# Fused dilated attention and mixture of experts on one core: ScalarE takes one of four masked key blocks, value products run in pairs of segments, one-hot rows come by a GpSimd transfer

## The chip, the core and the metric

The kernel runs on one core of a Trainium2 chip. The metric is the time of one execution on the device in microseconds. The core has five engines that matter here: TensorE (PE) multiplies, VectorE (DVE), ScalarE (ACT) and GpSimd (POOL) do element-wise work, and SyncE (SP) mostly issues transfers. Every engine runs its own instruction list strictly in order; semaphores tie the lists together.

## The reference, cut to what matters

The input is x, 4 batches of 512 tokens of width 128, in float32. Attention has 16 heads of width 8; tokens are put in a snake order, cut into 4 segments of 128, and each query sees every second key of its own segment, so 64 keys.

```python
x = x + layernorm(attn(layernorm(x), w_qkv, w_out))
x = x + layernorm(ffn(layernorm(x), ...))

# attn, per batch, head and segment
scores = einsum('bhsqd,bhskd->bhsqk', qh * scale, kd)   # 128 queries, 64 keys
o = einsum('bhsqk,bhskd->bhsqd', softmax(scores), vd)
return o_in_order @ w_out.T

# ffn: 8 experts, each token uses the best two, plus a shared gated path
combine = zeros.at[rows, topi].add(topw)
h = silu(einsum('nd,edf->nef', xf, w1)); ye = einsum('nef,efd->ned', h, w2)
return einsum('ne,ned->nd', combine, ye) + sigmoid(xf @ gate_w) * shared
```

All eight experts are computed for all tokens and weighted by `combine`.

## The kernel before, in words

The program is written as five instruction lists, one for each engine. Small functions emit one step for one batch `b` (and, in attention, for one segment `s` or one half of the heads); at the end of each engine's part a long hand-set sequence of calls fixes the order. Nothing is scheduled at run time: what stands first in an engine's list runs first, and a wait blocks all behind it.

Stages of one batch in attention:

- `x_T`, `k_project`, `q_project`, `values` (PE) project the normalised input. `k_high`/`q_high` (ACT) and `k_low`/`q_low` (DVE) split each projection in a high and a low part. For batches 1 to 3 SP places the parts on partitions 0 to 95 of `Ks` and `Qs` (`k_place`, `q_place`, L257 to L268).
- `k_blocks` (DVE, L1478 to L1486) multiplies `Ks` by a column of `cst` that is one for the rows of one head of a group and zero elsewhere; it does so four times a batch (`HG` is 4) and writes the masked key blocks `Kb`. Batch 0 uses `k_blocks_0` on two halves.
- `scores_q` (PE, L532) forms scores with queries on partitions; `maxima` (DVE, L1501) takes the negated row maxima from one PSUM bank of two; `max_split` (L1508, L1510) puts them in `Mq`; `max_T` (PE, L541) transposes them, and `max_rows` (ACT L1020, DVE L1493) writes them in rows 96 to 127 of `Qs`.
- `scores_k` (PE, L555) forms the scores again with keys on partitions. It uses all 128 rows: rows 96 to 127 of `Kb` are one-hot over the heads, so the product already holds score minus maximum. The one-hot rows are made by ACT (`key_ones`, L1094, in `kone`) and copied by SP into both halves of `Kb` (L274).
- `exps` (ACT, L1078) takes the exponential of one half's bank into one of four buffers `Pr`. `attend` (PE, L572) multiplies by the values for one segment: eight products on strips of 32 columns. `attended` (ACT, L1070) copies the 256 columns to `AVs`, `attend_T` (PE, L585) transposes them, and `divide` (DVE, L1517 and L1519) divides two segments at a time.
- `output_T`, `project` (PE), `y_copy` (ACT), statistics (DVE), powers and the residual `TR` (POOL) give the input of the second half.

In the second half PE runs `expert_h` (L443 to L445, three products for each hidden layer) and `expert_o` (L676) for eight experts and the shared path; for the last batch these are `last_h` and `last_o` (L731) on halves of the tokens. ACT applies SiLU and weights experts 1, 3, 5 and the shared path (`weight`); DVE adds the other experts (`accumulate`, L1619; `last_sum`, L1650); POOL adds ACT's parts (L377, L385) and computes exponentials of the router for batches 2 and 3 (`router_exp`, L332). Batches overlap: PE works on `scores_k` of one batch, `scores_q` of the next, and from batch 2 on the experts of batch 0.

The first steps of the program: ACT loads `cst`, makes the two parts of the selection matrix `sel` (L1212, L1213), then `kone` (L1094), and only then copies the first half of the transposed input (`x_copy_0`, L974).

## Time and profile before

| | us |
|---|---|
| median of 3 runs | 146.08 (145.68 to 146.86) |
| the profiled execution, as timed | 146.6 |
| its span, from the first to the last instruction | 144.8 |
| PE busy | 134.2 (93%) |
| DVE busy | 125.8 (87%) |
| ACT busy | 106.2 (73%) |
| POOL busy | 58.0 (40%) |

The profiled execution took 1.8 us more than its span, and 0.5 us more than the median. A PE instruction's shown duration reaches into the next one's, since matmuls are pipelined; the chain of waits, which lays pieces end to end, tells better what a group of matmuls costs. An idle time in brackets is what an engine waited before an instruction, with the one that released it.

### The profile page before, as it was taken

How to read it: one execution, taken by the hardware profiler on the slowest of the kernel's cores; microseconds unless marked ns; L12 is line 12 of the kernel's file. 1: busy time of each engine (PE TensorE's matmuls, PEld its weight loads, DVE VectorE, ACT ScalarE, POOL GpSimd, SP SyncE). 2: the span in 40 equal slices, each digit the busy share in tenths (PEclk: the TensorE clock that was granted, in tenths of full speed). 3: DMA queues.
4: the chain of work that ended last, by engine and by line, in shares of the span. 5: the costliest groups of instructions: out<-in, count | busy, mean ns of one | idle time of the engine just before them, and what ended most of it. 6: DMA issues, size and time to landing. Idle time of an engine off the chain costs nothing.

```text
span 144.8 us, 3566 instructions
## 1 busy us (share of the span) xinstructions
PE 134.2 (93%) x1142; PEld 117.0 (81%) x1142; DVE 125.8 (87%) x478; ACT 106.2 (73%) x264; POOL 58.0 (40%) x57
## 2 busy tenths in 40 slices
PE   6889988999999999999999999999999999999940
PEld 5578775887978688878889799999789899999930
DVE  6969999999899899979789684999999949999892
ACT  4569786876896478658989893675588777977670
POOL 7343023000039533704532009949533498305221
PEclk9999999999999999999999999999999999999996
DMA  4941089999993860000000000000000200020022
GB/s 139 264 108 38 32 172 136 247 181 158 196 302 114 142 77 5 0 0 7 0 2 5 0 0 0 5 2 0 0 2 5 72 2 2 2 71 5 0 72 72
DMA packets 13217, 9.54 MB, mean 66 GB/s; under 512 B 1040, under 2 KB 12048, under 8 KB 13200
## 3 DMA queue, kind: packets, MB, share of 16 engines
q1 hardware_dynamic: 12784, 9.12, 29.9%
q10 hardware_dynamic: 416, 0.21, 0.5%
q8 instruction: 9, 0.15, 0.4%
q14 instruction: 8, 0.07, 0.2%
HBM read 3.69 MB, written 1.05 MB: 33 GB/s over the span
## 4 chain that ended last, share of the span: by engine, by line
PE 76%; DVE 8%; ACT 5%; issue 4%; DMA 3%; POOL 1%; POOLq 1%; ACTq 0%; DVEq 0%
PE bank L676 14%; PE bank L555 10%; PE bank L532 7%; PE bank L443 6%; PE bank L572 6%; PE bank L445 5%; PE bank L444 5%; PE bank L731 4%; DMA cst<-in_consts 3%; PE bank L585 2%; PE bank L605 2%; PE bank L503 2%; PE bank L541 2%; DVE negm L1501 1%; PE bank L617 1%
## 5 line engine op out<-in xcount | busy, mean ns | idle before, releaser
L357 POOL TENSOR_TENSOR RS<-VE,nhalf 128x4 f32<-128x4 f32 x14 | 15.4, 1099 | 50.8 <-DVE VE L1405 50.8
L1501 DVE TENSOR_REDUCE negm<-bank 128x8 f32<-128x512 f32 x32 | 21.1, 686 | 1.8 <-PE bank L532 1.4
L1078 ACT ACTIVATE Pr<-bank 128x512 f32<-128x512 f32 x32 | 18.8, 600 | 4.0 <-PE bank L555 3.8
L1619 DVE SCALAR_TENSOR_TENSOR X<-bank,CW,X 128x128 f32<-128x128 f32 x60 | 16.7, 341 | 4.5 <-PE bank L676 4.5
L555 PE MATMUL bank<-Qs,Kb 128*128 128x128 f32 x128 | 19.3, 278 | 0.4 <-ACT Pr L1078 0.3
L555 PEld LDWEIGHTS bank<-Qs,Kb 128*128 128x128 f32 x128 | 16.7, 190 | 3.0 <-issue 1.6
L676 PEld LDWEIGHTS bank<-w2n,Pr 128*128 128x128 f32 x128 | 15.8, 191 | 0.9 <-issue 0.2
L443 PE MATMUL bank<-XH,w1h 128*128 128x512 f32 (+1 forms) x40 | 16.2, 406 | 0.2 <-ACT Pr L1143 0.2
L676 PE MATMUL bank<-w2n,Pr 128*128 128x128 f32 x128 | 16.4, 276 | 0.0
L332 POOL TENSOR_TENSOR EX<-base,DL 128x36 f32<-128x36 f32 x2 | 12.2, 6124 | 9.3 <-DVE DL L1554 9.3
L1158 ACT ACTIVATE Tm<-bank,CW 128x128 f32<-128x128 f32 x36 | 10.2, 370 | 6.6 <-PE bank L676 4.8
L532 PE MATMUL bank<-Kb,Qs 96*128 96x256 f32 x64 | 14.2, 318 | 0.1
L445 PE MATMUL bank<-XL,w1h 128*128 128x512 f32 (+1 forms) x40 | 14.0, 349 | 0.0
L444 PE MATMUL bank<-XH,w1l 128*128 128x512 f32 (+1 forms) x40 | 13.9, 349 | 0.0
L1143 ACT ACTIVATE Pr<-bank 128x512 f32<-128x512 f32 x19 | 11.2, 604 | 2.2 <-PE bank L445 1.4
L532 PEld LDWEIGHTS bank<-Kb,Qs 96*128 96x128 f32 x64 | 9.4, 189 | 2.1 <-issue 1.5
L572 PE MATMUL bank<-Pr,Vb 128*32 128x128 f32 x256 | 10.3, 279 | 0.1
L1070 ACT ACTIVATE AVs<-bank 128x256 f32<-128x256 f32 x16 | 6.2, 386 | 5.2 <-PE bank L572 5.2
L377 POOL TENSOR_TENSOR Tm<-Tm 128x512 f32<-128x512 f32 x6 | 7.7, 1277 | 4.7 <-ACT Tm L1158 4.6
L731 PE MATMUL bank<-w2n,Pr 128*128 128x128 f32 x64 | 8.8, 275 | 0.0
L443 PEld LDWEIGHTS bank<-XH,w1h 128*128 128x128 f32 x40 | 7.6, 190 | 1.3 <-ACT Pr L1143 0.6
L1484 DVE TENSOR_SCALAR Kb<-Ks,cst 96x1024 fp32r<-96x1024 f32 x12 | 8.3, 745 | 0.1
(155 smaller groups left out, 346.2 us busy)
## 6 DMA issues: line engine op xcount, KB each, us to landing
Qs<-qch SPq DMA_DIRECT2D x6, 256.0 KB, 5.5
Kb<-kone SPq DMA_DIRECT2D x8, 128.0 KB, 4.9
X<-in_L_attn_x SPq DMA_DIRECT2D x4, 256.0 KB, 6.3
XP<-in_x_snake SPq DMA_DIRECT2D x3, 256.0 KB, 4.3
Ks<-kch SPq DMA_DIRECT2D x6, 128.0 KB, 3.1
Qs<-qcl SPq DMA_DIRECT2D x3, 256.0 KB, 7.2
out<-XN SPq DMA_DIRECT2D x3, 256.0 KB, 2.2
w1n<-in_L_ffn_w SPq DMA_DIRECT2D x1, 512.0 KB, 8.7
```

The lines of the kernel that those rows point to most:

```text
L357: nc.gpsimd.tensor_tensor(RS[:, k, b], VE[:, k, b], nhalf[:], ALU.pow).then_inc(pw[k], 1)
L443: mm(out_, wh, vh, start=True, stop=False)
L444: mm(out_, wl, vh, start=False, stop=False)
L445: return mm(out_, wh, vl, start=False, stop=True)
L532: i = mm(S1[n % 2][:, j * 256:(j + 1) * 256], Qs[0:MROW, b % 2, g, s * P:(s + 1) * P], Kb[0:MROW, b % 2, g, s], start=True, stop=True)
L555: i = mm(S2[s2_bank(n)][:, j * P:(j + 1) * P], Kb[:, b % 2, g, s, 2 * pr:2 * pr + 2], Qs[:, b % 2, g, s * P:(s + 1) * P], start=True, stop ...
L572: i = mm(PC[j * VW:(j + 1) * VW, (s % 2) * 2 * P + half * P:(s % 2) * 2 * P + (half + 1) * P], Vb[:, b % 2, s, half * 4 + j], Pr[:, n % 4, ...
L676: i = mm(ps[output_bank(n, s)][:, s * P:(s + 1) * P], lhs[:, s * P:(s + 1) * P], w, start=True, stop=True)
L731: i = mm(ps[(6, 7, 5)[j]][:, s * P:(s + 1) * P], hs[:, j, c + s * P:c + (s + 1) * P], w2n[:, u % E], start=True, stop=True)
L1078: A(Pr[:, n % 4], bank(S2[s2_bank(n)], 4), ACT.Exp).then_inc(S["ex"], 1)
L1501: V.tensor_reduce(negm[:, b % 2, s, 8 * half:8 * half + 8], bank(S1[n % 2], 8, KEYS), AX.X, ALU.max, negate=True).then_inc(S["mx"], 1)
L1619: V.scalar_tensor_tensor(out=acc[:, b, t], in0=ps[output_bank(n)][:, t * P:(t + 1) * P], scalar=CW[:, b, t, k:k + 1], in1=acc[:, b, t], op ...
```

## The change

1. **One-hot rows.** `key_ones` on ACT, the tile `kone` and SP's eight copies are gone. The rows come as a new input `key_rows` in DRAM (32 rows of 16 KB) by two transfers that POOL issues: `key_heads(0)` behind `powers(0, 1)`, `key_heads(1)` behind `powers(0, 3)`, the second waiting for the placed queries of batch 1. `cst` is 16 columns narrower.
2. **Key blocks.** For batches 1 to 3 DVE makes three of the four blocks, and ACT the fourth (`k_block`), from the same `Ks`.
3. **Value products in pairs.** `attend`, `attended` and `attend_T` handle two segments at a time: 16 products in one run on a whole PSUM bank, one copy of 512 columns. `Pr` has six buffers for `exps` instead of four.
4. **Early loads.** On SP `w1n`, `woT` and `X` of batches 0 and 1 come ahead of `k_place(1)`.
5. **New orders** of the calls on all engines. In the start `x_T_0(1)` goes ahead of `qkv_0(0)`, and the second part of `sel` behind the first copy of the transposed input. At the end `finish(1)` (DVE) goes from between the sums of batch 2 to behind `norm_out(2)`, `finish_out(1)` (ACT) to behind `last_silu(10)`, and POOL's `powers(3, 1)` to behind `add_weighted(2)`.

```diff
+            def key_heads(u):
+                if u:
+                    pool.wait_ge(q_in[1], 16 * PARTS)
+                pool.dma_start(Kb[MROW:P, u].rearrange("p g s h k -> p (g s h k)"), key_rows).then_inc(kdma[u], 16)
...
-            key_ones(0)
+            sp.dma_start(w1n[:], w1.rearrange("e d f -> d e f")).then_inc(S["ld_w1"], 16)
+            sp.dma_start(woT[:], w_outT).then_inc(S["ld_wout"], 16)
+            for b in range(2):
+                sp.dma_start(X[:, b], x_v[b]).then_inc(ld_x[b], 16)
             k_place(1)
             q_place(1)
...
+            def k_block(b):
+
+                h = HG - 1
+                act.wait_ge(k_in[b], 16 * PARTS)
+                if b >= 2:
+                    act.wait_ge(S["s2"], 8 * (b - 1))
+                A(Kb[0:MROW, b % 2, :, :, h].rearrange("p g s k -> p (g s) k"),
+                  Ks[0:MROW].rearrange("p g (s k) -> p (g s) k", k=KEYS).bitcast(F32), ACT.Copy,
+                  scale=cst[0:MROW, C_HM + h:C_HM + h + 1]).then_inc(S["kb_a"], 1)
...
-            def k_blocks(b, heads=range(HG)):
+            def k_blocks(b, heads=range(HG - 1)):
...
-            def attend(b, s):
+            def attend(b, c):
...
-                if NT * b + s >= 1:
-                    pe.wait_ge(S["avc"], NT * b + s)
+                if 2 * b + c >= 1:
+                    pe.wait_ge(S["avc"], 2 * b + c)
...
+                for s in range(2 * c, 2 * c + 2):
+                    for half in range(2):
+                        n = (b * NT + s) * 2 + half
+                        pe.wait_ge(S["ex"], n + 1)
...
-            def attended(b, s):
-                n = NT * b + s
+            def attended(b, c):
+
+                n = 2 * b + c
                 act.wait_ge(S["pv"], n + 1)
                 if n >= 2:
                     act.wait_ge(S["at"], n - 1)
-                A(AVs[:, s % 2], PC[:, (s % 2) * 2 * P:(s % 2 + 1) * 2 * P], ACT.Copy).then_inc(S["avc"], 1)
+                A(AVs[:, c], PC[:], ACT.Copy).then_inc(S["avc"], 1)
...
-                    if n >= 4:
-                        act.wait_ge(S["pv"], (n - 4) // 2 + 1)
-                    A(Pr[:, n % 4], bank(S2[s2_bank(n)], 4), ACT.Exp).then_inc(S["ex"], 1)
+                    if n >= 6:
+                        act.wait_ge(S["pv"], (n - 6) // 4 + 1)
+                    A(Pr[:, n % 6], bank(S2[s2_bank(n)], 4), ACT.Exp).then_inc(S["ex"], 1)
```

The first place is ACT's list behind the load of the constants. Before:

```order
L1212 ACTIVATE sel<-cst 128x4x64
L1213 ACTIVATE sel<-cst 128x4x2x32
L1094 ACTIVATE kone<-cst 32x1024
L974 ACTIVATE xT<-bank 128x256
L979 ACTIVATE kch<-bank 128x128
```

and in the changed kernel:

```order
L957 ACTIVATE sel<-cst 128x4x64
L963 ACTIVATE xT<-bank 128x256
L957 ACTIVATE sel<-cst 128x4x2x32
L963 ACTIVATE xT<-bank 128x256
L968 ACTIVATE kch<-bank 128x128
```

Two copies have left the place ahead of the first `xT`, one of them for good.

The second place is PE's list where batch 0 goes over to batch 1; L555 and L557 are `scores_k`, L532 and L534 `scores_q`, L572 and L575 `attend`, L585 and L587 `attend_T`. Before:

```order
L555 MATMUL bank<-Qs,Kb 128x128 x12
L572 MATMUL bank<-Pr,Vb 32x128 x8
L555 MATMUL bank<-Qs,Kb 128x128 x4
L532 MATMUL bank<-Kb,Qs 128x256 x4
L555 MATMUL bank<-Qs,Kb 128x128 x4
L572 MATMUL bank<-Pr,Vb 32x128 x8
L532 MATMUL bank<-Kb,Qs 128x256 x2
```

and in the changed kernel:

```order
L557 MATMUL bank<-Qs,Kb 128x128 x16
L534 MATMUL bank<-Kb,Qs 128x256 x4
L557 MATMUL bank<-Qs,Kb 128x128 x8
L534 MATMUL bank<-Kb,Qs 128x256 x2
L575 MATMUL bank<-Pr,Vb 32x128 x16
L534 MATMUL bank<-Kb,Qs 128x256 x4
```

The first value products stand behind six products of `scores_q` and all of segment 2's `scores_k`, and are twice as many in one run.

The third place is ACT's list behind the first `max_rows` (L1020, L1009). Before:

```order
L1020 ACTIVATE Qs<-bank 32x512 x2
L1078 ACTIVATE Pr<-bank 128x512 x3
L1038 ACTIVATE kch<-bank 128x256
L1070 ACTIVATE AVs<-bank 128x256
L1078 ACTIVATE Pr<-bank 128x512
```

and in the changed kernel:

```order
L1009 ACTIVATE Qs<-bank 32x512 x2
L1035 ACTIVATE Kb<-Ks,cst 96x16x64
L1027 ACTIVATE kch<-bank 128x256
L1078 ACTIVATE Pr<-bank 128x512 x5
L1018 ACTIVATE qch<-bank 128x512
```

The new key block and the high part of the keys of batch 2 stand ahead of the first exponential.

## Rows read from the trace of the kernel before

**Rows 1.** The page: busy time and share of each engine.
```profile
PE 134.2 (93%) x1142; PEld 117.0 (81%) x1142; DVE 125.8 (87%) x478; ACT 106.2 (73%) x264; POOL 58.0 (40%) x57
```

**Rows 2.** Busy time by stretch; columns in the first line.
```profile
core 0: us, PE busy (x) PEld busy (x) DVE busy (x) ACT busy (x) POOL busy (x), PEclk, DMA share, GB/s
0.00:8.00 8.00, 5.22 (x15) 3.76 (x15) 6.31 (x27) 4.14 (x6) 4.21 (x16) 1.00 0.64 183
8.00:22.00 14.00, 13.21 (x92) 11.21 (x92) 12.80 (x35) 11.44 (x29) 4.05 (x5) 1.00 0.43 92
22.00:35.00 13.00, 12.27 (x130) 9.53 (x131) 12.31 (x31) 9.29 (x21) 1.01 (x1) 1.00 1.06 186
35.00:66.00 31.00, 30.58 (x323) 26.14 (x323) 28.32 (x77) 23.04 (x49) 11.76 (x11) 1.00 0.52 103
66.00:85.00 19.00, 19.00 (x190) 16.53 (x188) 15.55 (x79) 17.02 (x42) 5.86 (x5) 1.00 0.01 2
85.00:139.00 54.00, 53.81 (x399) 49.80 (x398) 47.43 (x222) 39.67 (x116) 30.34 (x19) 1.00 0.04 11
139.00:144.80 5.80, 0.10 (x1) 0.00 (x0) 3.06 (x13) 1.61 (x6) 0.83 (x1) 0.77 0.30 90
```

**Rows 3.** The chain of waits in the start: start us, us, what.
```profile
6.43 1.05 ACT kone L1094
```

**Rows 4.** Timeline of the start: start us, us, instruction, idle before it.
```profile
8.78 0.29 DVE L1423 TENSOR_TENSOR kcl<-bank,kch 128x128 fp32r<-128x128 f32 x1 [1.09 <-ACT kch L979]
```

**Rows 5.** The chain of waits around the first transposed maxima and the first exponential.
```profile
21.40 0.69 DVE Mq L1510
...
24.65 0.61 ACT Pr L1078
25.26 0.14 issue
25.40 0.63 PE bank L555 x4
...
34.55 0.24 DVE Mq L1510
34.79 0.04 issue
34.83 0.66 PE bank L541 x4
```

**Rows 6.** The chain of waits around value products at 57 to 61 us.
```profile
57.10 0.40 PE bank L555 x4
57.50 0.57 PE bank L572 x16
58.08 0.43 PE bank L532 x2
...
61.10 0.59 PE bank L555 x4
61.69 0.29 PE bank L532 x2
```

**Rows 7.** The page's costliest groups: key blocks and the copies behind value products.
```profile
L1070 ACT ACTIVATE AVs<-bank 128x256 f32<-128x256 f32 x16 | 6.2, 386 | 5.2 <-PE bank L572 5.2
L1484 DVE TENSOR_SCALAR Kb<-Ks,cst 96x1024 fp32r<-96x1024 f32 x12 | 8.3, 745 | 0.1
```

**Rows 8.** Timeline: an ACT copy of 1024 columns, and two PE waits on divided sums and copies.
```profile
41.38 1.10 ACT L1111 ACTIVATE w1h<-w1n 128x1024 fp32r<-128x1024 f32 x1
47.89 0.65 PE L572 MATMUL bank<-Pr,Vb 128*32 128x128 f32 x16
48.76 0.41 PE L585 MATMUL bank<-cst,AVs 128*128 128x128 f32 x2 [0.22 <-DVE O L1519]
```

**Rows 9.** Timeline of POOL: powers and key columns around the place of the new transfer.
```profile
7.77 1.01 POOL L357 TENSOR_TENSOR RS<-VE,nhalf 128x4 f32<-128x4 f32 x1 [1.82 <-DVE VE L1405]
10.00 0.64 POOL L323 COPY xk<-xT 128x512 f32<-128x512 f32 x1 [1.22 <-ACT xT L974]
21.36 0.64 POOL L323 COPY xk<-xT 128x512 f32<-128x512 f32 x1 [2.06 <-PE bank L515]
```

**Rows 10.** Timeline of the end: the last products, POOL's router exponential and DVE.
```profile
137.59 1.50 PE L731 MATMUL bank<-w2n,Pr 128*128 128x128 f32 x12
115.17 6.12 POOL L332 TENSOR_TENSOR EX<-base,DL 128x36 f32<-128x36 f32 x1
121.70 1.19 DVE L1562 TENSOR_SCALAR EZ<-EX 128x4 f32<-128x4 f32 x1
119.62 0.87 DVE L1687 SCALAR_TENSOR_TENSOR X<-X,RS,TR 128x128 f32<-128x128 f32 x3
```

More of the change, by code:

```diff
@@ L421, in _ @@
             add_weighted(1)
-            powers(3, 1)
             router_exp(3)
             add_weighted(2)
+            powers(3, 1)
             powers(3, 2)
@@ L670, in outputs @@
                 elif n < E + 4:
[L672 removed]
+                    pe.wait_ge(*((S["sh"], made(0, E - 1)[1]), (S["avc"], 2 * B), (S["oTs"], B))[n - E - 1])
                 else:
@@ L821, in _ @@
             project(1)
+            scores_k(2, 1, (1,))
+            scores_k(2, 2, (0,))
             attend(2, 0)
-            scores_k(2, 1, (1,))
             scores_q(3, 0)
+            scores_k(2, 2, (1,))
+            scores_q(3, 1, (0,))
             moe_in(0)
-            scores_k(2, 2, (0,))
-            scores_q(3, 1, (0,))
+            scores_q(3, 1, (1,))
+            scores_k(2, 3)
+            scores_q(3, 2)
             attend_T(2, 0)
-            scores_k(2, 2, (1,))
+            router(0)
+            scores_q(3, 3, (0,))
             attend(2, 1)
-            scores_q(3, 1, (1,))
-            scores_k(2, 3, (0,))
+            scores_q(3, 3, (1,))
+            gate(0)
             attend_T(2, 1)
-            scores_q(3, 2, (0,))
-            router(0)
-            scores_q(3, 2, (1,))
-            attend(2, 2)
-            scores_k(2, 3, (1,))
-            scores_q(3, 3, (0,))
-            attend_T(2, 2)
-            scores_q(3, 3, (1,))
-            attend(2, 3)
-            gate(0)
-            attend_T(2, 3)
+            up(0)
             max_T(3)
-            up(0)
             output_T(2)
@@ L969, in _, with selection @@
             act.dma_start(cst[:], consts).then_inc(S["ld_cst"], 16)
+            def selection(j):
+                act.wait_ge(S["ld_cst"], 16)
+                act.wait_ge(S["selz"], 1)
+                A(sel[:, :, 4:8:2] if j else sel[:, :, 0:2], ident.rearrange("p (c g) -> p g c", g=G).unsqueeze(2)
+                  .to_broadcast([P, G, 2, 32]), ACT.Copy).then_inc(S["selr"], 1)
             def x_copy_0(h):
@@ L1090, in x3_high @@
                 A(XH[:, b], x3_bank(b)[:], ACT.Copy).then_inc(S["x3h"], 1)
-            def key_ones():
-                A(kone[MROW:P], cst[MROW:P, C_ONE:C_ONE + G * HG].rearrange("p (g h) -> p g h", g=G).unsqueeze(3)
-                  .to_broadcast([P - MROW, G, HG, KEYS]), ACT.Copy).then_inc(S["kones"], 1)
             def router_high():
@@ L1318, in _ @@
-            weight(0, 1)
-            attended(3, 3)
+            x3_high(1)
+            exps(3, 2, (1,))
+            tanh(3)
+            attended(3, 0)
+            exps(3, 3, (0,))
+            weight(0, 1)
+            exps(3, 3, (1,))
+            router_exp(1)
+            silu(0, 4)
+            normalise_3(2, (0, 1))
+            attended(3, 1)
+            silu(0, 5)
+            normalise_3(2, (2, 3))
+            weight(0, 3)
             x3_high(2)
-            silu(0, 4)
-            silu(0, 5)
@@ L1745, in _ @@
             max_rows(0)
-            k_blocks(1)
+            k_blocks(1, (0, 1))
+            k_low(2)
+            k_blocks(1, (2,))
             neg_mean(0, 3)
-            k_low(2)
             maxima(1, 0)
+            maxima(1, 1, (0,))
             q_low(2)
-            maxima(1, 1)
+            maxima(1, 1, (1,))
             maxima(1, 2)
@@ L1869, in _ @@
             below_largest(3)
+            add_other(1)
+            norm_out(1)
             accumulate(2, 0)
+            finish(0)
             accumulate(2, 2)
-            finish(1)
             accumulate(2, 4)
@@ L1887, in _ @@
             norm_out(2)
+            finish(1)
             last_sum(2)
@@ L1915, in constants @@
         c[:MROW, C_HM + h] = (p[:MROW] % 32) // HD == h
-    for h in range(H):
-        c[MROW:, C_ONE + h] = (p[MROW:] - MROW) % H == h
     for j in range(2):
@@ L1922, in constants, with head_rows @@
     return c
+def head_rows():
+    import numpy as np
+    p = np.arange(P - MROW).reshape(-1, 1, 1, 1, 1) % H
+    head = np.arange(H).reshape(1, G, 1, HG, 1)
+    rows = np.zeros((P - MROW, G, NT, HG, KEYS), np.float32)
+    rows[:] = p == head
+    return rows.reshape(P - MROW, -1)
 def snake_order():
```

488 lines of the change are left out of this document (219 added, 269 removed), and 2 rows, old and new, of the table names.

## The prediction, made before the changed kernel was run

> **What bounds the kernel now.** I read busy time first. PE is busy for 134.2 us of a span of 144.8, DVE for 125.8, ACT for 106.2 [rows 1]: two engines are nearly full. Shares over the span hide the stages, so I cut it [rows 2]. From 66 us to 139 PE has 0.2 us of idle time in 73, at a granted clock of 1.00, while DVE, ACT and POOL have slack: there the end is set by how much PE has to do, and the change gives PE the same products. From 139 on PE is done and 5.8 us of sums, statistics and stores remain. So whatever the change gains must be gained before about 66 us, be kept by a PE that stays full, or come from work that PE spends between products. Before 66 us PE has idle time (2.8 us to 8 us, 0.8 us to 22, 0.7 to 35, 0.4 to 66), and DVE is about as full: 12.80 of 14, 12.31 of 13, 28.32 of 31. In that part DVE's maxima gate PE and PE's scores gate DVE, so a gain on one alone is worth only part of itself. That this change takes work from both is what makes it promising.
>
> The sum is made against the profiled execution: span 144.8, timed at 146.6. The median of the runs is 146.08, 0.5 lower, and what comes out is set against that. About 1% (1.5 us) is the least that a measurement can tell from no change.
>
> **The change, part by part.**
>
> *One-hot rows and the start.* The chain of waits runs through the load of the constants, both `sel` copies, then the `kone` copy of 1.05 us [rows 3]. It goes, and one `sel` copy moves behind the first `xT` copy. But the transpose that feeds `xT` is released by the same constants, and DVE is nearly full from 8 us on [rows 2]; the idle time it can give back is the 1.09 us in which it waited for the first high keys [rows 4]. Everything later in the start is DVE work that stays. Bounds: 0, if another engine's order (ACT now has three input normalisations ahead of steps that it had behind) eats it, and −1.1. I take −0.5, near the middle, since ACT is also busy for 11.44 of 14 us there [rows 2] and has the moved copy still to do.
>
> SP's eight copies of these rows go too, and POOL issues two transfers. The trace has no transfer issued by POOL. From below: it costs POOL nothing, since POOL had gaps of 1.82 and 1.22 us at that place [rows 9]. From above: it holds POOL as long as its nearest rows, a power of 1.01 and a copy of 0.64 us, together 1.7 us, and then the powers of batch 2 come late for DVE. Rows are needed at about 24 us, when the first `scores_k` runs [rows 5], 15 us after the issue. I take 0 and keep +0.5. What speaks against the transfer is seen in a row: DVE's small subtraction into `Mq` took 0.69 us at 21.40, while POOL's copy of the key columns ran from 21.36 to 22.00, and 0.24 at 34.55 without it [rows 5, 9]. DVE and POOL do lock each other out. The Trainium skill (SBUF — State Buffer, section SBUF: two separate sides) goes further: descriptors of a GpSimd transfer are written through the port pair that DVE's two-port operations hold, so such a transfer starves beside a busy DVE. By that rule the rows land late, as a rival below; by the row each collision costs at most one instruction, some 0.5 us, and the margin of 15 us covers it.
>
> *Key blocks.* DVE loses three operations (one for each of batches 1 to 3) of 745 ns [rows 7]: −2.2 us of DVE. ACT gains three. Nearest row: an ACT copy of 1024 columns from SBUF takes 1.10 us [rows 8]; so +3.3 us of ACT, against −1.05 for `kone`. The Trainium skill (ScalarE: Activation LUTs, section What ACT_TABLE_LOAD costs) adds about 93 ns for a scale given by pointer, as here; three times that is 0.3 us of an engine with slack, and the sum would be the same. Where the block stands decides. In batch 1 it is ahead of the first exponential, with the high keys: ACT's list there is two rows of maxima, block, high keys, exponential. The first exponential began at 24.65 and PE stood waiting for it until 25.40 [rows 5]; 1.10 for the block and about 0.3 for the keys put it 1.4 us later, less the 0.5 from the start. So PE stands about 0.9 us longer at that place, while `scores_q(1, 0)`, which waits for all blocks of batch 1, can start 0.7 us sooner and has no value products ahead of it; the maxima of batch 1 then begin sooner by that and by the start. To the end of this stretch at 35 us I count −0.5 (DVE's −0.74, minus a part lost to the exponentials); bounds +0.9 and −1.0.
>
> *Pairs.* Value products use strips of 32 columns, all others the whole array. The cost of going over shows in the chain: 16 records take 0.57 us, though four rounds at the pitch of `scores_k` (0.40 for four) would be 0.40 to 0.45; and the group behind is longer, `scores_q` 0.43 against 0.29, `scores_k` 0.59 against 0.40 [rows 6]. So a run of value products carries 0.12 to 0.17 of its own and 0.14 to 0.19 behind it, about 0.3 us. Eight of the sixteen runs disappear. I take 0.25 for each, a little low, because a gap of the chain next to a transpose can be a wait. Six of them lie behind 35 us, where PE is full: −1.5. Two lie before, where DVE is the tighter side, and are in the −0.5 above. Bounds: 0, where a later pair only turns it into a wait, and −2.4 for all eight at 0.3.
>
> The copies change from sixteen of 386 ns to eight of 512 columns, 600 ns by the exponentials of that size: −1.4 us of ACT. ACT's balance is then +0.9 us over the whole span; in 22 to 66 us it had 11.7 us of slack [rows 2].
>
> *Waits between copy and transposes.* At 47.89 and 48.76 PE's next group waited for a copy and for a division [rows 8]; four copies in a row per batch become two with other work between them. I take −0.3, bounds 0 and −0.8.
>
> *Early loads, end.* The loads move out of 22 to 35 us, where transfers filled more than one share of the engines (1.06 [rows 2]); no compute engine was shown waiting for them: 0. At the end `finish(1)` takes its four updates and two small operations, some 1.4 us (0.87 for three updates [rows 10]), from about 119 us to about 130, into a DVE that is full there. Against that, POOL's router exponential of 6.12 us no longer stands behind `powers(3, 1)`, and the 1.19 us that DVE's `EZ` took, its POOL neighbour still running [rows 10], may go. I take 0, bounds +1.0 and −0.5.
>
> Sum: −0.5 −0.5 −1.5 −0.3 = −2.8 us. The profiled execution would come to 143.8, the median to **143.3 us**. Everything after 66 us should only be shifted; PE's last product then ends near 136.3 instead of 139.09 [rows 10].
>
> **Rivals.**
>
> *More is gained (141.8 or below).* The start gives its 1.1 us, pairs 2.4, waits 0.8, batch 1's stretch 1.0: −5.3 at the very most, 140.8. For it: DVE and PE are relieved in the same places. Against it: all covers would have to be perfect. Chance 0.10.
>
> *The gain is given back (within 1%).* PE arrives early in the experts and now waits there for router weights, for POOL's additions or for maxima. For it: DVE is busy for 15.55 of 19 us and ACT for 17.02 of 19 in 66 to 85 [rows 2], and the exponentials are bunched by the pairs. If half of the gain is lost, the time is 144.7; if nearly all, 146. Chance 0.24.
>
> *ACT starves the pairs (slower).* A pair needs four exponentials, two of them in one go behind a new key block, and everything behind it on PE stands. Each of the eight pairs may wait; what is gained by other parts is 2.8 us, so 0.35 us a pair cancels it, and 0.55 a pair makes it slower by over 1%. With 0.65 a pair, as long as one exponential (0.61 [rows 5]), the time is 143.3 + 5.2 = 148.5. For it: ACT is the fullest of the helpers at 66 to 85. Against it: six buffers instead of four, and other products in between. Chance 0.07.
>
> *The one-hot rows land late.* If the transfer starves until DVE's dense stretch ends, it would land after the first `scores_k` at 24 us, and each microsecond beyond is one microsecond of PE: landing at 28 us gives 143.3 + 4 = 147.3. This is what the page on SBUF would bring. For it: DVE is busy for 12.80 us of 14 from 8 to 22. Against it: the lock is let go between instructions [rows 5, 9], and maxima read PSUM. Chance 0.03.
>
> *The order does not do what it says*, for instance PE's early pieces stand at other semaphores: this falls in the second case.
>
> **The numbers.** The forecast has 0.56, the further gain 0.10, given back 0.24, starving 0.07, late rows 0.03. Faster by over 1% (below 144.6): the first two and a little of the third, 0.69. Within 1%: 0.23. Slower by over 1% (above 147.5): 0.08. The range leaves out the slower cases and a tail of the second and third: 141.6 to 145.9.
>
> **What the profile of the changed kernel would show.** The start: the first projection about 0.9 us earlier than 7.94, DVE's first wait of 1.09 nearly gone, and the first transposed maxima some 0.5 us earlier than 22.14. Pairs: a run of 32 records at about 0.9 to 1.0 us in the chain, not 1.14. Key blocks: nine DVE operations and three ACT ones of 1.1 to 1.2 us, and a PE wait for the first exponential near 26 us of about 1 us. PE full from 66 us on and done near 136.3, with 5.8 us behind it. The prediction is wrong if ACT's exponentials end PE's idle time in many places, if `kb_a` or the row transfer releases a PE instruction, or if PE shows idle time in the experts.

## The result, and the profile after

The changed kernel is **slower**: 150.09, 150.40, 156.84 and 156.86 us, against 145.94 us (145.68 to 146.86) for the kernel before on the same chip. The executions fall into two groups by their mean granted clock, 0.97 and 0.93, and every ratio in this document compares the faster group of each kernel: here 1.0284, interval 1.0203 to 1.0364. The forecast was 143.3 us. The profiled execution took 150.4, span 148.6.

Two words are used below. A *stand* is a time in which PE has no instruction that may start; a *fall* is a stretch in which the granted clock of PE is at the lower of its two levels, 1.2 GHz instead of 2.4.

First the page: tenths of each slice in which PE was busy, and the granted clock of PE (each slice 3.7 us).

```profile
PE   6999977999999999599999999999999999999940
PEclk9999999659999999999999999999999999999996
```

Two marks stand out: a 6 and a 5 in the clock (26 to 33 us), and a 5 of PE's busy time near 60 us. The same in stretches, columns as in [rows 2]:

```profile
22.00:35.00 13.00, 11.78 (x89) 10.07 (x88) 8.26 (x21) 8.14 (x15) 1.98 (x3) 0.74 0.62 105
50.00:66.00 16.00, 13.81 (x160) 12.39 (x158) 15.21 (x41) 11.92 (x24) 8.33 (x7) 1.00 0.37 50
82.00:140.00 58.00, 57.74 (x457) 53.90 (x456) 49.61 (x235) 44.46 (x122) 30.13 (x18) 1.00 0.03 10
```

From 22 to 35 us the clock was 1.00 in [rows 2] and is 0.74 now. From 82 us on PE is as full as it was. So the loss lies before about 67 us, in two places. Milestones say how much (the same step of PE in both traces, before and after): first transposed maxima 22.14 and 21.84, `scores_q(1, 0)` 27.17 and 27.11, `values(2)` 35.32 and 37.69, third transposed maxima 49.13 and 51.99, the first product of the experts 62.94 and 67.38, end of PE 139.09 and 142.86 us. The lead is 0.3 us at 22 us; 2.4 us are lost between 27 and 37 us, 0.5 up to 52, 1.6 up to 67; 0.7 come back; at the end 3.8 are missing.

**The first place: the clock.** Timeline of the changed kernel, PE and ACT (start us, us, instruction, idle before it):

```profile
21.84 0.55 PE L543 MATMUL bank<-cst,Mq 128*128 128x128 f32 x3 [0.84 <-DVE Mq L1493]
23.63 1.15 ACT L1035 ACTIVATE Kb<-Ks,cst 96x1024 fp32r<-96x1024 f32 x1
24.81 0.38 ACT L1027 ACTIVATE kch<-bank 128x256 fp32r<-128x256 f32 x1
25.09 1.08 ACT L1078 ACTIVATE Pr<-bank 128x512 f32<-128x512 f32 x2
25.82 1.12 PE L557 MATMUL bank<-Qs,Kb 128*128 128x128 f32 x8 [1.06 <-ACT Pr L1078]
27.11 1.22 PE L534 MATMUL bank<-Kb,Qs 96*128 96x256 f32 x4 [0.17 <-DMA Qs<-qcl]
30.40 1.94 PE L575 MATMUL bank<-Pr,Vb 128*32 128x128 f32 x32
```

ACT makes its key block, then the high keys, then the exponential for which PE waits: 1.06 us where it was 0.33. That is the wait the prediction named. It had not asked what the wait does to the clock: the granted clock is full until 26.9 us, then at its lower level, 1.2 GHz, until 33.7 us, for 6.8 us. The run of 32 value products takes 1.94 us in there, and 1.01 at full clock (below). In the trace before, the clock stays full from the start to 142 us. The milestones compare two different lists; the same list at full clock is in run 1 below. From `scores_q(1, 0)` to `values(2)` it takes 7.58 us there (26.48 to 34.06) and 10.58 here, so this fall costs 3.0 us.

**The second place: VectorE stands beside GpSimd.** Timeline of POOL, DVE and PE around 60 us:

```profile
55.67 1.95 POOL L350 TENSOR_TENSOR RS<-VE,nhalf 128x4 f32<-128x4 f32 x1 [4.98 <-DVE VE L1388]
57.61 2.36 POOL L309 TENSOR_TENSOR w1l<-w1n,w1h 128x1024 fp32r<-128x1024 f32 x1
57.65 2.34 DVE L1429 SCALAR_TENSOR_TENSOR NM<-MV,RS 128x4 f32<-128x4 f32 x1
60.03 1.65 ACT L1085 ACTIVATE X<-TR,NM,RS 128x128 f32<-128x128 f32 x4 [1.66 <-DVE NM L1429]
61.17 1.28 DVE L1484 TENSOR_REDUCE negm<-bank 128x8 f32<-128x512 f32 x2
62.00 0.47 PE L534 MATMUL bank<-Kb,Qs 96*128 96x256 f32 x2 [1.82 <-DVE negm L1484]
```

A product of 128x4 that takes 0.15 us elsewhere takes 2.34, for as long as POOL subtracts `w1l` in 2.36 us. I call this the lock: the short instruction of one engine lasts until the long one of the other ends. Behind the held product follow statistics and the row maxima that free PE's bank: PE waits 1.82 us. `experts_low()`, which issues that subtraction, was moved behind `powers(2, 0)`; and the operation that needs the result of `powers(2, 0)` is this very `neg_mean(2, 0)`. Both start as soon as the power ends. That power is itself slow: 1.95 us beside three key blocks of DVE, where most powers of its size take 1.01. In the trace before, the subtraction ran beside maxima and divisions that DVE reads from PSUM, and no instruction of DVE grew by more than 0.1 us:

```profile
46.37 2.36 POOL L316 TENSOR_TENSOR w1l<-w1n,w1h 128x1024 fp32r<-128x1024 f32 x1
```

That was close: the next cast between SBUF tiles started at 48.52, only 0.2 us before the subtraction ended.

**What came as forecast.** A pair's run and the group behind it, from the chain of waits:

```profile
66.09 1.01 PE bank L575 x32
67.10 0.43 PE bank L534 x2
```

The changed groups, busy us and mean ns of one:

```profile
L1070 ACT ACTIVATE AVs<-bank 128x512 f32<-128x512 f32 x8 | 4.8, 596 | 5.7 <-PE bank L575 5.7
L1467 DVE TENSOR_SCALAR Kb<-Ks,cst 96x1024 fp32r<-96x1024 f32 x9 | 6.4, 747 | 0.1
L1035 ACT ACTIVATE Kb<-Ks,cst 96x1024 fp32r<-96x1024 f32 x3 | 3.4, 1147 | 0.1
```

Against [rows 6, 7]: 1.01 us for 32 records instead of twice 0.57; eight copies of 596 ns; nine blocks on DVE and three of 1.15 us on ACT. The issue of the new transfers, with the first wait of DVE (it was 1.09 in [rows 4]):

```profile
8.39 0.29 DVE L1406 TENSOR_TENSOR kcl<-bank,kch 128x128 fp32r<-128x128 f32 x1 [0.49 <-ACT kch L968]
8.94 0.72 POOL L384 DMA_DIRECT2D Kb<-in_key_rows  x1
27.37 0.58 POOL L384 DMA_DIRECT2D Kb<-in_key_rows  x1 [3.23 <-DMA Qs<-qcl]
```

The transfers themselves (KB each, median us from issue to landing):

```profile
Kb<-in_key_rows POOLq DMA_DIRECT2D x2, 512.0 KB, 5.7
```

So the rows of the first transfer were there at 15 us, nine before they are needed.

### The profile page after: what moved, and what is told of

Its sections match the earlier page's. It is cut to its first block, busy times and chain, and to the rows that moved or that the text cites. A ratio compares the mean times of both kernels' runs of the same rounds, so it can differ in the third digit from the quotient of the medians.

```text
span 148.6 us, 3553 instructions
## 1 busy us (share of the span) xinstructions
PE 135.4 (91%) x1142; PEld 120.7 (81%) x1142; DVE 124.6 (84%) x475; ACT 108.1 (73%) x258; POOL 59.5 (40%) x59
## 4 chain that ended last, share of the span: by engine, by line
PE 70%; DVE 11%; DMA 4%; issue 4%; ACT 3%; SPq 3%; POOL 2%; POOLq 1%; DVEq 0%; ACTq 0%
PE bank L678 15%; PE bank L557 7%; PE bank L534 6%; PE bank L444 6%; PE bank L575 5%; PE bank L445 5%; PE bank L446 5%; DMA Qs<-qcl 4%; PE bank L441 4%; PE bank L733 3%; PE bank L587 2%; DVE X L1602 2%; PE bank L607 2%; SPq L256 2%; DVE NM L1429 2%
## 5 line engine op out<-in xcount | busy, mean ns | idle before, releaser
L1078 ACT ACTIVATE Pr<-bank 128x512 f32<-128x512 f32 x32 | 18.2, 600 | 4.0 <-PE bank L557 3.7
L557 PE MATMUL bank<-Qs,Kb 128*128 128x128 f32 x128 | 19.2, 285 | 1.1 <-ACT Pr L1078 1.1
L557 PEld LDWEIGHTS bank<-Qs,Kb 128*128 128x128 f32 x128 | 17.6, 203 | 2.8 <-issue 1.4
L534 PE MATMUL bank<-Kb,Qs 96*128 96x256 f32 x64 | 15.1, 342 | 2.7 <-DVE negm L1484 2.0
L1138 ACT ACTIVATE Pr<-bank 128x512 f32<-128x512 f32 x19 | 11.2, 601 | 6.5 <-PE bank L446 6.2
L534 PEld LDWEIGHTS bank<-Kb,Qs 96*128 96x128 f32 x64 | 10.4, 211 | 6.3 <-issue 4.7
L316 POOL COPY xk<-xT 128x512 f32<-128x512 f32 x4 | 2.6, 656 | 24.4 <-ACT xT L1001 15.7
L1153 ACT ACTIVATE Tm<-bank,CW 128x128 f32<-128x128 f32 x36 | 10.2, 368 | 1.1 <-PE bank L678 1.1
L575 PE MATMUL bank<-Pr,Vb 128*32 128x128 f32 x256 | 9.5, 294 | 0.0
L1070 ACT ACTIVATE AVs<-bank 128x512 f32<-128x512 f32 x8 | 4.8, 596 | 5.7 <-PE bank L575 5.7
L678 PE MATMUL bank<-w2n,hs 128*128 128x128 f32 x64 | 8.5, 279 | 0.0
```

The lines of the kernel that those rows point to most:

```text
L534: i = mm(S1[n % 2][:, j * 256:(j + 1) * 256], Qs[0:MROW, b % 2, g, s * P:(s + 1) * P], Kb[0:MROW, b % 2, g, s], start=True, stop=True)
L557: i = mm(S2[s2_bank(n)][:, j * P:(j + 1) * P], Kb[:, b % 2, g, s, 2 * pr:2 * pr + 2], Qs[:, b % 2, g, s * P:(s + 1) * P], start=True, stop ...
L575: i = mm(PC[j * VW:(j + 1) * VW, (2 * (s % 2) + half) * P:(2 * (s % 2) + half + 1) * P], Vb[:, b % 2, s, half * 4 + j], Pr[:, n % 6, j], s ...
L678: i = mm(ps[output_bank(n, s)][:, s * P:(s + 1) * P], lhs[:, s * P:(s + 1) * P], w, start=True, stop=True)
L1078: A(Pr[:, n % 6], bank(S2[s2_bank(n)], 4), ACT.Exp).then_inc(S["ex"], 1)
```

## Experiments

Diffs are against the kernel named; times are medians in us with lowest and highest, each beside the kernel before on the same chip (145.9 to 146.2). In the profiled executions a mean clock of 0.99 or more goes with no fall before PE's last products, and one of 0.98 or less with one or two.

**1. Filler on PE.** One microsecond of products that nobody reads, where PE stood near 25 us.

```diff
 # the changed kernel, TensorE
             scores_k(0, 0)
+            warm_up(2, TH, PC)
             scores_k(0, 1)
```

> The changed kernel with two more filler products of 256 columns (into the bank that is free there) on PE between scores_k(0, 0) and scores_k(0, 1), where PE had stood 1.06 us for ACT's first exponential. Theory A (PE's idle time before 26 us let the granted clock fall to half from 26.9 to 33.7 us): the clock stays at its full level there, PE finishes about half of 6.8 us sooner, 147.0 us (146.4 to 147.6). Theory B (the clock falls for another reason, or the loss of 3.8 us lies in waits that have nothing to do with it): 150.1 us or a little more.

Measured: 147.77, 147.80 at a mean clock of 0.99, and 151.54, 151.67 at 0.96. In the profiled execution (147.77) the clock is full from 4 to 144 us, and the second place is unchanged:

```profile
54.98 2.38 POOL L309 TENSOR_TENSOR w1l<-w1n,w1h 128x1024 fp32r<-128x1024 f32 x1
55.02 2.35 DVE L1430 SCALAR_TENSOR_TENSOR NM<-MV,RS 128x4 f32<-128x4 f32 x1
59.38 0.48 PE L534 MATMUL bank<-Kb,Qs 96*128 96x256 f32 x2 [1.85 <-DVE negm L1485]
```

More work for PE makes the kernel 2.5 us faster (147.8 against 150.2). It is less than the 3.0 us of the fall, because PE, now earlier, meets two other waits: 0.49 us at 36.72 for a copy of ACT and 0.72 at 40.61 for a transfer of `Qs`. The second loss stays as it was, so the two are separate places; while the second is there, two of four executions still take some 3.8 us more at the lower mean clock.

**2 and 3. GpSimd's order, without and with the filler.**

```diff
 # the changed kernel, GpSimd
-            powers(2, 0)
             router_low()
             experts_low()
+            powers(2, 0)
 # 3: also the filler of 1
```

> The changed kernel with POOL's router_low and experts_low ahead of powers(2, 0), as before the change. Theory A (DVE's neg_mean(2, 0) was locked out by POOL's subtraction of 2.36 us and so held the maxima and PE, 1.82 us): neg_mean(2, 0) takes 0.15 us, PE no longer waits at 62 us, and 1.8 us are gone: 148.4 us. Theory B (the lock only uncovers a delay that some other wait brings anyway, or PE's end hangs elsewhere): less than 0.5 us gained, 149.7 or more. The granted clock should still fall near 27 us by both.

> The changed kernel with both edits, the filler products and POOL's old order. If the clock and the lock are two independent losses, they add: 145.0 us, a little below the kernel before (145.9). If one of them covers the other, 146.5 or more.

Measured: 2 has 146.71 to 147.38 in five executions of twelve (clock 0.99; ratio 1.0061 [1.0033, 1.0089]) and 151.32 to 152.25 in seven (0.955); 3 has 147.03 and 147.18 at clocks of 1.00 and 0.99, and 148.17 and 148.77 at 0.98, ratio 1.0128 [1.0064, 1.0192]. At full clock 3 is 0.7 us below the filler alone and far from the 145.0 that was expected, and its trace shows why:

```profile
47.52 2.35 POOL L309 TENSOR_TENSOR w1l<-w1n,w1h 128x1024 fp32r<-128x1024 f32 x1
47.59 2.30 DVE L1430 SCALAR_TENSOR_TENSOR NM<-MV,RS 128x4 f32<-128x4 f32 x1
50.31 0.66 PE L543 MATMUL bank<-cst,Mq 128*128 128x128 f32 x4 [1.83 <-DVE Mq L1494]
```

The subtraction now meets `neg_mean(1, 0)`, which the changed order of DVE has put ahead of `max_split(2)`; the trace of 2 has the same pair at 51.10 and 51.17. It was taken in an execution of 152.13 us and has two falls, one of 6.8 us behind the stand near 26 us, one of 3.4 behind the stand of 1.83 at 53.89. The clock held in five executions of 2 though its stands near 26 us are those of the changed kernel: the stands make a fall likely, they don't fix it.

**4. A later first exponential in the kernel before.** One ACT copy of 1024 columns into a tile that nobody reads, ahead of `exps(0, 0)`: the delay of the key block without the rest of the change.

```diff
 # the kernel before, ScalarE
             max_rows(0, (0, 1))
+            A(junk[0:MROW], ..., ACT.Copy)     # 1024 columns
             exps(0, 0)
```

> The kernel before with one copy of 1024 columns (into a tile nobody reads) on ACT between max_rows(0) and the first exponential, where the changed kernel has its key block. Theory A (the block ahead of the first exponential makes PE idle, and that brings the clock down): the clock falls near 27 us for about 7 us and the time goes from 145.9 to about 149.5. Theory B (the clock falls only with other parts of the change): the time rises by at most the copy's 1.1 us, to 147.0, and the clock stays at its full level.

Measured: 146.10 (145.87 to 148.47, ten executions), ratio 1.0007 [0.9981, 1.0033]. PE waits 0.67 us instead of 0.33, the clock stays full. A delay of this size costs nothing; run 8 doubles it. (The one execution at 148.47 has a clock of 0.98. Of 71 executions of the kernel before on record four are like it, 148.1 to 148.6 us, and none is below 0.98.)

**5. As 3, with `neg_mean(1, 0)` back behind `spread_y(2)`.**

```diff
 # the kernel of 3, VectorE
-            neg_mean(1, 0)
             max_split(2)
 ...
             spread_y(2)
+            neg_mean(1, 0)
```

> The kernel of e3_filler_and_pool with DVE's neg_mean(1, 0) out of its new place ahead of max_split(2), back behind spread_y(2). Theory A (whichever small DVE operation on two SBUF inputs meets POOL's subtraction of 2.36 us is held for its whole length, and in front of the maxima that costs PE): neg_mean(1, 0) takes 0.15 us there, PE's wait of 1.8 us for Mq at 50 us goes, and the time falls by 1.8 us to 145.3. Theory B (the division or the copies behind it are late anyway): at most 0.5 us gained, 146.6.

Measured: 146.77, 146.78, 146.85, 147.16 and 148.29 at a clock of 0.99 or more, and 148.73 to 149.21 in the other five (0.976); ratio 1.0085 [1.0037, 1.0132]. The lock moved to the next operation of DVE between tiles of SBUF:

```profile
48.25 2.35 POOL L309 TENSOR_TENSOR w1l<-w1n,w1h 128x1024 fp32r<-128x1024 f32 x1
48.44 2.21 DVE L1492 CAST Mq<-negm 128x64 fp32r<-128x64 f32 x1
```

A cast of one source, 0.18 us otherwise (49.81 in run 3), waits as long, PE stands 1.75 us behind it, and in this execution the clock falls for 3.4 us at 51.5. Taking away the instruction that was hit is no repair; the subtraction itself has to stand elsewhere.

**6. The end as before.** The kernel of 5 with `powers(3, 1)` ahead of `router_exp(3)`, and `finish(1)`, `finish_out(1)` and `combine(3)` at their old places.

```diff
 # the kernel of 5, VectorE (and the same for GpSimd's powers and ScalarE's store)
             accumulate(2, 2)
+            finish(1)
 ...
-            combine(3)
             accumulate(2, 6)
+            combine(3)
```

> The kernel of e5_and_mean_late with the orders of the end as before the change: POOL's powers(3, 1) ahead of router_exp(3), DVE's finish(1) between the sums of batch 2 and combine(3) behind the next sum, ACT's finish_out(1) ahead of last_silu(0). Theory A (the new end costs the 0.4 us that PE waits for DVE's sum near 128 us and delays behind it): 0.5 to 0.9 us less than e5_and_mean_late, about 144.6. Theory B (the end is set by PE's product count alone): within 0.2 us of e5_and_mean_late.

Measured: 150.17, 150.48, 150.52 and 152.54, ratio 1.0348 [1.0257, 1.0438]. With these lists PE stands 2.13 us near the end for `gated(3)`, and the clock falls behind it (two slices of 0.7 on the page at about 128 us):

```profile
127.71 1.87 PE L678 MATMUL bank<-dwn,Pr 128*128 128x128 f32 x8 [2.13 <-DVE Pr L1693]
```

So with these lists the old end is worse than the new one, by about 2 us (medians 150.5 and 148.5), and the new end is not where the change loses.

**7. Key block behind the exponential.** `k_block(1)` and `k_high(2)` behind `exps(0, 0)`, with GpSimd's order of 2 and DVE's of 5, no filler.

```diff
 # ScalarE
+            exps(0, 0)
             k_block(1)
             k_high(2)
-            exps(0, 0)
```

> The kernel of e5_and_mean_late without filler products, and with ACT's k_block(1) and k_high(2) behind exps(0, 0) instead of ahead of it. If the block's place ahead of the first exponential is what makes PE idle, PE loses its 1.06 us, the clock holds and the time is about 145.3. If PE's new order is (nothing stands between scores_k(0, 1) and scores_q(1, 0), since the value products have moved behind them), the idle time only moves to the front of scores_q(1, 0), which waits for the blocks and for the placed queries at 27.1 us; the clock falls to half for 6.8 us and the time is about 148.5.

Measured: 149.50 and 150.68 (clock 0.98), 152.39 and 153.71 (0.954). The stand only moves, from the first exponential to the key blocks behind it, and the clock falls right behind it (28.94 to 32.35 us) and once more at 52.8, behind a stand of 1.76:

```profile
24.79 1.12 PE L557 MATMUL bank<-Qs,Kb 128*128 128x128 f32 x8 [0.33 <-ACT Pr L1078]
27.65 0.72 PE L534 MATMUL bank<-Kb,Qs 96*128 96x256 f32 x4 [1.74 <-DVE Kb L1467]
```

**8. Run 4 with two copies.**

```diff
 # the kernel before, ScalarE
+            A(junk[0:MROW], ..., ACT.Copy)
+            A(junk2[0:MROW], ..., ACT.Copy)
             exps(0, 0)
```

> The kernel before with two copies of 1024 columns on ACT between max_rows(0) and the first exponential, 2 us in all. One copy left PE 0.84 + 0.67 us of idle time between 20 and 28 us and the clock held; the changed kernel had 2.3 us and it fell. With two copies PE should have 0.84 + 1.7 us. Theory A (idle time of PE in this stretch brings the clock down, whatever makes it): the clock falls to half near 27 us for about 7 us, and the time is about 149.5. Theory B (it is something else in the changed kernel): the clock holds, 147.5 at most.

Measured: 146.99 and 148.17 at a clock of 0.99, 151.43 and 151.56 at 0.96. The profiled execution (148.17) has PE wait 1.62 us at 27.21 and no fall. Two of four executions at 0.96, some 4 us dearer, where none of the 71 of the unchanged kernel is below 0.98: a longer stand at this place is enough to bring the fall in the kernel before too. Where it lies in those two executions is not profiled.

**9. `experts_low()` at a place where DVE reads PSUM, with the filler.**

```diff
 # the changed kernel, GpSimd
-            powers(2, 0)
             router_low()
-            experts_low()
+            powers(2, 0)
             powers(1, 1)
             add_rows(1)
+            experts_low()
 # and the filler of 1
```

> The changed kernel with 1 us of filler products between the two parts of scores_k(0), and on GpSimd router_low before powers(2, 0) and experts_low after add_rows(1), so that its 2.35 us subtraction should run near 61 us beside VectorE's maxima of PSUM. Theory (the lock between VectorE and GpSimd costs the 1.8 us for which TensorE waited for Mq in the third run): no instruction of VectorE before 66 us takes over 1 us more than its kind, the wait is gone, and the time is 147.1 - 1.8 = 145.3 us. Rival (the subtraction meets the next operation of VectorE between tiles of SBUF wherever it stands): again one row about 2 us too long and 146.6 us or more. PE's granted clock full after the start in both.

Measured: 145.76 (145.41 to 146.65, ten executions), ratio 0.9986 [0.9965, 1.0006]. The subtraction runs beside maxima, and none of them grows:

```profile
59.78 1.28 DVE L1485 TENSOR_REDUCE negm<-bank 128x8 f32<-128x512 f32 x2
59.82 2.37 POOL L309 TENSOR_TENSOR w1l<-w1n,w1h 128x1024 fp32r<-128x1024 f32 x1
61.36 0.42 DVE L1503 TENSOR_TENSOR O<-bank,rden 128x256 f32<-128x256 f32 x1
```

The same instruction, as long as before, costs 2.0 us less (147.8 to 145.76) by standing 5 us later, and all ten executions keep the clock (0.99 or more). What is left is small waits on ACT's copies and a transfer:

```profile
33.89 0.66 PE L587 MATMUL bank<-cst,AVs 128*128 128x128 f32 x4 [0.29 <-ACT AVs L1071]
36.80 0.38 PE L607 MATMUL bank<-woT,oT 128*128 128x128 f32 x1 [0.25 <-ACT oT L1044]
48.96 0.63 PE L543 MATMUL bank<-cst,Mq 128*128 128x128 f32 x4 [0.22 <-ACT AVs L1071]
```

**10. Run 9 with every pair split.**

```diff
 # the kernel of 9, TensorE, at each of the eight pairs
+            attend(0, 0, (0,))
             # the piece that stood ahead of the pair
-            attend(0, 0)
+            attend(0, 0, (1,))
```

> The kernel of the run before this, with each of the eight pairs of value products put back into two runs, one before and one after the piece that stands ahead of the pair; the copies and the waits for them stay as they are. If a switch of runs costs what the prediction took, 0.25 us, this is 8 x 0.25 = 2.0 us slower than the run before it. If the switch costs nothing (the gap ahead of a run is hidden by the next products), the two are within 0.4 us, and the 1.5 us that the prediction took from the pairs was never there.

Measured: 148.43 (148.28 to 148.60), ratio 1.0153 [1.0131, 1.0176]: 2.67 us more than 9 for eight more runs of value products, 0.33 for each where the prediction took 0.25. In its chain of waits:

```profile
28.33 0.57 PE bank L575 x16
28.91 0.43 PE bank L534 x2
29.34 0.57 PE bank L575 x16
```

**11. Run 9 with all key blocks by VectorE.**

```diff
 # the kernel of 9
-            k_block(1)                 # ScalarE, and (2), (3)
-            k_blocks(1, (2,))          # VectorE, likewise for 2 and 3
+            k_blocks(1, (2, 3))
```

> The kernel of the first run of this group with the fourth masked key block of batches one to three made by VectorE again (three blocks of 0.75 us) instead of ScalarE (three of 1.15 us). The prediction took 0.5 us for the block of batch 1. If VectorE is what ends last before the scores of batch 1, this is 0.5 to 1 us slower than the first; if ScalarE's 1.15 us ahead of the first exponential is what holds the stretch, it is as fast or up to 1 us faster.

Measured: 145.41 (145.20 to 147.44, five executions), ratio 0.9968 [0.9927, 1.0010]. The filler now hides the whole wait for the first exponential, and PE waits 0.57 us for the transfer of `Qs` instead. ScalarE's block is worth nothing; undoing it ends PE 0.45 us sooner, and the intervals of 9 and 11 overlap.

**12. No filler; a segment of value products in its place.** GpSimd as in 9, ScalarE as in 7, DVE's block (1, 2) before `k_low(2)`.

```diff
 # TensorE
-            scores_k(0, 1)
+            scores_k(0, 1, (0,))
+            attend(0, 0, (0,))
+            scores_k(0, 1, (1,))
 # and attend(0, 0, (1,)) where the pair was
```

> The changed kernel without any filler: GpSimd's order as in the first run of this group, ScalarE's block of batch 1 behind exps(0, 0), VectorE's block (1, 2) before k_low(2), and the first segment of attend(0, 0) between the two parts of scores_k(0, 1), where TensorE had stood. Theory (the fall of the clock comes from TensorE's stand near 26 us, and the lock costs 1.8 us): granted clock full from 7 to 139 us and 145.3 us or less. Rival (the stand only moves, as it did with the block behind the exponentials alone): a stand of over 0.8 us between 24 and 30 us and a stretch at half clock of about 3.4 us behind it, 148 us or more.

Measured: 146.16 (145.44 to 149.75, ten executions), ratio 1.0005 [0.9983, 1.0027]. PE's wait near 25 us is 0.33 us again, and nine of ten executions have a clock of 0.99 or more (one 0.96, at 149.75). Nearly the same effect as the filler, with work that has to be done anyway; the 145.3 expected was not reached.

**13. All repairs, key blocks by VectorE, no filler** (12 with the edit of 11).

> The twelfth run's kernel (GpSimd's order repaired, the first segment of attend(0, 0) between the two parts of scores_k(0, 1), no filler) with all four key blocks of every batch made by VectorE. The ScalarE block was worth -0.35 us in the eleventh run against the ninth, so: 146.2 - 0.4 = 145.8 us, and as low as 145.2 if the stand near 25 us goes as well. Rival (VectorE's third and fourth block end later than ScalarE's did once there is no filler, so TensorE stands before scores_q(1, 0)): 146.5 us or more.

Measured: 145.93 (144.79 to 146.30, twelve executions) against 146.01; ratio 0.9962 [0.9935, 0.9990]. The best version is 0.1 to 0.65% faster than the kernel before by the interval, less than 1%.

**14. GpSimd's order of 9 alone.** No filler.

> The changed kernel with GpSimd's order alone repaired (router_low before powers(2, 0), experts_low after add_rows(1)). If the lock costs 1.8 us by itself and the clock's fall is a separate loss: half clock for 3.4 to 6.8 us near 27 us still, no row of VectorE 2 us too long, and 150.1 - 1.8 = 148.3 us (its lowest executions). If the two losses are one (the lock only appears because TensorE fell behind): 150 us or more, or full clock without any filler.

Measured: 149.00, 150.71, 150.71 and 150.73. No row of DVE is too long, PE waits 1.1 us for the exponential, and the clock is at its lower level from 27.91 us for 10.24 us:

```profile
PEclk9999999755899999999999999999999999999997
```

Against 9 this is the filler by itself: 1 us of work that nobody needs is worth 3.2 to 5.0 us. The first theory holds in kind; its 148.3 us were missed, since the fall was longer than in the changed kernel (10.2 us, not 6.8), and three of four executions are no faster than the changed kernel's 150.1 and 150.4. So what the lock costs is read from 1 against 9 and from 15, where the clock held, not from here. No execution is near 156.8.

**15. The move of `experts_low()` alone, in the kernel before.**

```diff
 # the kernel before, GpSimd
-            experts_low()
             powers(2, 0)
+            experts_low()
```

> The kernel before with experts_low behind powers(2, 0) instead of ahead of it on GpSimd, and nothing else. If the lock is what the move costs: neg_mean(2, 0), 0.16 us long near 51.8 us, takes 2.2 to 2.4 us beside the subtraction's 2.36, the four key blocks behind it start 2.2 us later, and the time is 147.0 to 148.3 us. If a move on GpSimd alone is harmless (the prediction's cost of at most 0.5 us): 146.0 to 146.5 us.

Measured: 147.43, 147.62, 148.65 and, with a clock of 0.94, 155.39 and 156.06; ratio 1.0129 [1.0072, 1.0186]. The profiled execution is one of the last two and shows both losses in a row. Timeline of POOL, DVE and PE:

```profile
51.00 2.58 POOL L316 TENSOR_TENSOR w1l<-w1n,w1h 128x1024 fp32r<-128x1024 f32 x1
51.44 2.16 DVE L1446 SCALAR_TENSOR_TENSOR NM<-MV,RS 128x4 f32<-128x4 f32 x1
53.52 2.73 DVE L1484 TENSOR_SCALAR Kb<-Ks,cst 96x1024 fp32r<-96x1024 f32 x4
55.05 0.43 PE L572 MATMUL bank<-Pr,Vb 128*32 128x128 f32 x8 [1.08 <-ACT Pr L1078]
```

The stretch behind it, columns as in [rows 2]:

```profile
57.00:74.00 17.00, 17.00 (x107) 14.55 (x106) 9.42 (x27) 6.64 (x14) 3.97 (x4) 0.50 0.00 0
```

One line moved by one place on an engine that is busy for 40% of the span costs 1.6 us at full clock (the middle of the three executions at 0.99, 147.62, against 146.01), and 9 to 10 us when the clock goes with it. PE was busy for all of the 17 us from 57 to 74, at half the clock.

## Why the prediction was wrong

**The step that failed first** is "PE stands about 0.9 us longer". The wait was foreseen, at its place and nearly in its size (1.06 us measured for about 1), and then priced as time alone. The sum took a granted clock of 1.00 over from the trace before. The clock cost 3.0 us in the profiled execution (10.58 us for steps that take 7.58 at full clock in run 1), three times the stand itself; the filler brings the clock back (9 against 14, and two of four executions of run 1), a longer stand in the kernel before brings the fall in two of four executions (run 8), and moving the stand does not help (run 7). The Trainium skill (TensorE: Matmul & The Clock Gate, section HAM oscillation — how this bites in real kernels) tells of a kernel whose waits between bursts of products drop TensorE to the slow clock, so that each next burst starts slow. The trace agrees in kind, and stands of 0.84 and 1.06 us, shorter than the waits of that kernel, were enough here.

**The second** is "each collision costs at most one instruction, some 0.5 us". It is one instruction, but it lasts as long as GpSimd's: 2.34 us beside 2.36. The row it was taken from (0.69 us [rows 5], beside a copy of 0.64 [rows 9]) says the same when read so: the length of the collision was that of the copy. And the prediction looked for collisions only at the new transfer; it never followed `experts_low` across `powers(2, 0)`, though the diff shows it and every instruction that a step is moved past counts. The Trainium skill (SBUF — State Buffer, section SBUF: two separate sides) says of the shared pair of ports that whoever starts first has it "for the whole instruction; the other fully blocks". By that sentence and the 2.36 us of the subtraction in the trace before, less the 0.15 of the product, an estimate of +2.2 us would have stood in the sum. Traces agree for operations of DVE with two SBUF inputs and for a cast with one (2.21 us, run 5), and operations that read PSUM run free (run 9). Cost at full clock: 2.0 us (1 against 9), 1.6 us in the kernel before (15).

**The sum once more.** Run 9 has neither loss, so its 145.76 is what is left of the forecast: 2.5 us short of it, and 0.2 better than before.
- Start, −0.5: not shown, and smaller if anything. The first projection came 0.5 us sooner (7.43), not 0.9, the first wait of DVE fell from 1.09 to 0.49, and the first transposed maxima came 0.3 us sooner than 22.14. But that step stands at 21.38 to 22.65 in the four traces with the old start, always 16.9 us behind the first `sel` copy and so behind the load of the constants, and at 21.48 to 22.24 in the thirteen with the new start. The means are 22.0 and 21.8.
- One-hot rows by GpSimd, 0: right; no engine waited for them.
- Key block on ScalarE, −0.5 in the stretch: wrong. With both losses repaired it is worth +0.35 (9 against 11), about nothing.
- Pairs, −1.5: the switch was a little underpriced, 0.33 us instead of 0.25 (run 10), and only a part of it is kept (below).
- Waits between copy and transposes, −0.3: wrong sign. The copy of a pair begins when all 32 records are done and takes 0.6 us; the transposes behind it wait. Between 27 and 139 us the trace before has two waits of PE of over 0.15 us, 0.4 us in all; run 9 has seven, 1.65 in all, two of them (0.51) for such a copy.
- Early loads, 0: no wait for one of these loads shows. But the transfer of `Qs`, for which PE never waits in the trace before, makes it wait 0.17 us near 27 us in the changed kernel, 0.57 in run 11, and near 40 us 0.24 in run 9, 0.48 in run 12 and 0.72 in run 1.
- The new end, 0 with −0.5 to +1.0: the run with the old end is about 2 us slower, but as one of a group of lists made to fit each other; by itself this isn't shown.

Milestones show where the pairs' gain went. Run 9 leads the kernel before by 0.38 us at `scores_q(1, 0)`, by 0.18 at the first product of the experts (62.76), and by 0.85 at the last group of products (136.74 against 137.59). So the two pairs behind 63 us, where PE is full, bring 0.67 us, twice the 0.33 of run 10: there the prediction's term holds. The six before bring 2.0 by the same price; longer waits take 1.2 of that, and the lead still shrinks by 0.2. That leaves 1.0 us in no single wait, not settled; part of it may be that run 10 puts its split segments at other places than the kernel before.

**The rivals.** None had the mechanism. Starving pairs had the right engine for the first stand but the wrong price, and late rows were refuted; the two together had a chance of 0.10, and two other losses decided. Also wrong: "PE shows idle time in the experts" as a sign; PE's stretch from 82 us on is as full as before.

**Open.** Not profiled is an execution of the changed kernel at 156.8 us. Its mean clock is 0.93, the traces of runs 2, 5 and 7 have a fall that begins 0.2 to 0.9 us behind a stand of 1.75 to 1.83 us made by the lock, run 15 has one of 17 us, and runs 9 and 14 have no such execution. All this makes a second fall behind the 1.82 us stand at 62 us likely; it is argued, not shown. Why one execution of a program falls and the next does not stays open too.

## What to carry to other kernels

Price a new stand of TensorE twice: its length, and what the clock does behind it; where the new list has a hole near others, fill it with due work (run 12), or with anything (run 1). Before a long GpSimd operation between SBUF tiles is moved, look up what VectorE does in its new window: beside reads of PSUM it was free, beside the product and the cast between SBUF tiles that it met here it cost nearly its full length. An engine busy for 40% of the span can hold the one that decides: the two places together cost 4.5 us (150.2 against 145.76), more than the whole forecast gain of 2.8.

## What the runs showed of the hardware

- A 0.15 us operation of DVE lasts as long as the POOL operation that it starts beside: 2.34 beside 2.36, 2.30 beside 2.35, and a one-source cast 2.21 beside 2.35. Maxima from PSUM beside the same POOL operation keep their 0.64 to 0.69 us. It works the other way too: a POOL power of 1.01 us took 1.95 beside three key blocks of DVE.
- The granted clock fell to its lower level behind stands of 0.84 and 1.06 us that lay 4 us apart, with small gaps between; with 0.84 and 0.67 us at the same places (run 4) its mean was 0.99 in nine of ten executions, with 0.84 and 1.62 (run 8) in two of four. The same program fell in some executions and not in others (2: seven of twelve).
- A fall lasted 3.4, 6.8, 10.2 or 17 us, while PE was busy throughout in the longest (17.00 of 17 us, run 15); 6.8 us of it cost 3.0.
- A switch to products on strips of 32 columns and back costs 0.33 us (run 10 against 9, eight of them).
- A transfer of 512 KB issued by GpSimd beside a dense DVE landed 5.7 us after its issue; the issue held POOL for 0.58 and 0.72 us.
